# At a step's boundary the waiting probabilities are split ahead of Q's last evacuation; sums of the ffn weights, loads of x and splits of the first tiles are moved

## The chip, the cores and the metric

One core of a Trainium2 chip runs the whole program. The time is the device time of one execution in microseconds; lower is better. The number to predict is the median over runs of the changed kernel, timed on the same chip as the kernel before. Engines are called PE (matmuls), PEld (its weight loads), ACT, DVE, POOL and SP (SP only issues transfers and waits).

## What is computed

The reference, cut to what matters (B = 8 batches of S = 512 rows, D = 1024, 16 heads of 64):

```python
q, k, v = proj(x, Wq), proj(x, Wk), proj(x, Wv)      # float32, per head
q = q * minimum(cond_1, 4.0)
scores = einsum('bhqd,bhkd->bhqk', q, k) / 8.0
attn = softmax(where(causal, scores, finfo.min))
o = einsum('bhqk,bhkd->bhqd', attn, v)  # then heads side by side
y = einsum('bsd,ed->bse', o, Wo)
scale_x = maximum(max(abs(y), axis=-1), 1e-5) / 127
q_x = clip(round(y / scale_x), -128, 127) * scale_x
alpha = maximum(mean(abs(weight)), 1e-5)
q_w = clip(round(weight / alpha), -1, 1) * alpha
return x + einsum('bsi,oi->bso', q_x, q_w) + bias
```

## The kernel before

All float32 matrices are split in two parts ("high" is the value rounded by ACT to the multiplier's format, "low" is what is left, written by DVE or POOL), and each product is made of three matmul passes. So every operand costs a high operation on ACT and a low one on DVE or POOL before PE may use it. The order of the instructions on each engine is written out by hand; engines meet in semaphores, each engine takes its own instructions strictly in order, and SP issues every transfer but one in the order in which it is written.

**Stage V** (to 333 us) computes V for all rows. Pairs of row tiles n = 0 and 1 are done plainly; n = 2 to 15 are done in seven products each (A11, S4, A12, S2, S1, S3, A22, in this order on PE, 12 matmuls each, function `v_product`). PSUM bank `bank_z` is used by A12, then S1, then A22: S1 waits until DVE has added A12's result (`v_sum(n, 0)`), A22 waits for ACT's copy of S1's (`v_copy(.., V_TMP_R)`). S3 waits for the copy `V_TMP_U`. Beside the products of pair n, ACT and DVE split the seven operands of pair n + 1 (`xv_split`: B11, B22, B21, T2, T1, T3, T4), and DVE's `v_sum(n, 0)` stands behind its low parts of B11 and B22. Results go to HBM by `store_v`; the high part `v_high(n, q)` waits until the store that last used its slot has landed.

In the same stage the ffn weight is made ternary. SP loads its eight slices (`load_wf`, 512 KB each, two buffers): slices 0 and 1 at the end of pair 2, slices 2 and 3, 4 and 5, 6 and 7 at the end of pairs 3, 4 and 5, each time behind the pair's last `store_v`. ACT sums their absolute values (`wf_abs`, two at the end of each of the pairs 3 to 6); PE adds over the partitions (`wf_add_partitions`, line 942, in pair 7 behind A11); DVE forms alpha (`wf_scale`) and then rounds one slice a pair in three operations (`wf_ternary`, parts 0 to 2), which are spread over the pair's DVE work. At the end of pair 15, ACT also splits Wq's and Wk's first group and the eight slices of the first x tile (`x_high(act, 0, k)`).

**Stage A** (333 to 1600 us) has 32 steps, 4 groups of 4 heads by 8 batches, and a closing one. A step's PE program (`pe_step`) projects K and Q for the step `now` (`J(gi, k)`, four groups K0, Q0, K1, Q1 of 8 slices, lines 174) and between them does scores `S(u)`, transposes `T(u)` and products with V `PV(h)` of 16 units u = (head, row tile), some of the step `old`, the later ones of `now`. A unit goes: S(u) on PE, mask and row minimum on DVE (`M`, line 254), exponential on ACT (`E`, line 261), reciprocal on DVE (`I`), normalising on POOL (line 273), T(u) on PE, then the transposed probabilities are split, high on ACT (`H`, line 297) and low on DVE (`L`, line 304). T(u) waits for L(u - 2), since there are two PSUM banks.

The **boundary** of a step: PE ends a step with S(5), T(2), J(3, 7) and starts the next with S(6), T(3), J(0, 0..1), S(7), T(4), J(0, 2..3), S(8), T(5). J(3, 7) completes Q1; at the head of the next step ACT copies it out in two halves with the scale (`evac_hi(act, o, 3)`, line 204), DVE writes its low parts (`evac_lo(dve, o, 3)`, line 219) and the next scale (`batch_scale`), and behind these stand H(2) and L(2). S(8) is the first unit of the second head pair: it waits for these evacuations and for `k_sw`, the copy of K1 with the halves swapped, which SP makes by two transfers (`swap_k(.., 1)`, lines 229 and 230). SP issues them at the head of its step, behind `store_o(.., 1)` of the step that ended, which waits for the last addition of the output, OA(3) on DVE. The x slices of the next step are split at the end of a step: ACT 0 to 5 in three pairs (4 and 5 as the step's last work), DVE 0, 2, 4, POOL 1, 3, 5 behind units 2, 3 and 4; slices 6 and 7 follow inside the next step. `load_x` is issued behind `swap_k(.., 1)` of each step; in the very first step, which has no `old`, it is the first thing SP issues, ahead of the swap of K0 (`swap_k(.., 0)`) for which S(0) waits.

**Stage F** (from about 1600 us) multiplies with Wo, quantises, transposes and multiplies with the ternary weight, 32 row tiles. The first two tiles' splits (`o_high`, `o_low_part`), Wo's slices (`wo_high`, `wo_low`) and part of their products (`YY(k)`, `Y`) lie inside the last steps of stage A.

## Time and profile before

| | |
|---|---|
| median of 3 runs | 2084.48 us (2084.17 to 2085.92) |
| the profiled execution's own time | 2085.09 us |
| its span in the profile | 2083.3 us, mean granted clock of PE 0.994 of full speed |
| PE busy | 1991.5 us (96%) |
| DVE, ACT, POOL busy | 1416.1, 1114.4, 888.4 us |
| idle time of PE in stage A at T(4), behind DVE's L(2) | about 1.26 to 1.74 us in most steps |
| time from one boundary to the next | 38.4 to 38.7 us in most steps |

Busy times say which engine is near its limit over the whole; what a change of order can bring is read from PE's idle time and from what ended it, and at each place from the time at which the next thing in the chain becomes ready. In the rows, an instruction's line gives its start and length in us, its engine and line, what it writes and reads, and in brackets how long the engine had been idle before it and who ended that. `x12` are twelve instructions merged into one row.

### The profile page before, as it was taken

The page shows a single profiled execution, that of the slowest core. Times are in us where ns is not written, and L with a number is a line of the kernel's source. Part 1 is how long each engine was busy: PE and PEld are TensorE (multiplying, and loading weights), DVE is VectorE, ACT ScalarE, POOL GpSimd, SP SyncE. Part 2 cuts the span into 40 slices and gives each one's busy share as a digit, 9 for nine tenths or more (in the row PEclk, how much of TensorE's full clock was granted, in tenths as well). Part 3 has the DMA queues.
Part 4 walks back from the last instruction along what each step waited for, and adds up shares of the span by engine and source line. Part 5 has one row for each costly group of instructions (what it writes and reads, how often), then busy time and mean ns, then how long its engine had stood idle before and what let it go on. Part 6 is the DMA issues. An engine that isn't in the chain of part 4 may idle for free.

```text
span 2083.3 us, 34749 instructions
## 1 busy us (share of the span) xinstructions
PE 1991.5 (96%) x10074; PEld 1617.8 (78%) x10074; DVE 1416.1 (68%) x3277; ACT 1114.4 (53%) x2497; POOL 888.4 (43%) x816
## 2 busy tenths in 40 slices
PE   8999998999999999999999999999997999999998
PEld 6877886788788788787788787787886777777775
DVE  6667774777778777778777778777777554545454
ACT  4554444777767677768777778777775000000000
POOL 0343332544444444444444445444444544444442
PEclk9999999999999999999999999999999999999999
DMA  6666555333453443453433443433443423232322
GB/s 206 222 220 210 200 176 181 122 125 101 146 156 102 135 128 101 144 159 102 147 116 106 151 151 103 151 110 111 146 147 96 146 91 121 91 121 91 121 91 81
DMA packets 200981, 282.43 MB, mean 136 GB/s; under 512 B 11216, under 2 KB 146384, under 8 KB 199760
## 3 DMA queue, kind: packets, MB, share of 16 engines
q1 hardware_dynamic: 200384, 281.07, 42.8%
q8 instruction: 34, 0.56, 0.1%
q10 hardware_dynamic: 528, 0.52, 0.1%
q14 instruction: 35, 0.29, 0.0%
HBM read 178.79 MB, written 69.21 MB: 119 GB/s over the span
## 4 chain that ended last, share of the span: by engine, by line
PE 72%; DVE 10%; issue 6%; ACT 6%; DMA 3%; POOL 1%; DVEq 0%; SPq 0%; ACTq 0%; POOLq 0%
PE proj_ps L174 24%; PE proj_ps L509 8%; PE s_ps L509 8%; PE o_ps L317 6%; PE o_ps L580 5%; PE t_ps L870 5%; PE t_ps L283 5%; PE o_ps L870 3%; PE s_ps L243 2%; PE s_ps L242 2%; DVE q_st L219 2%; ACT parts L359 2%; DVE prob L254 2%; DVE parts L365 1%; ACT prob L261 1%
## 5 line engine op out<-in xcount | busy, mean ns | idle before, releaser
L174 PE MATMUL proj_ps<-parts 128*128 128x512 f32 x3072 | 840.9, 408 | 0.0
L273 POOL TENSOR_TENSOR prob<-prob,row_inv 128x128 f32<-128x128 f32 (+3 forms) x512 | 387.6, 757 | 696.2 <-DVE row_inv L267 691.2
L174 PEld LDWEIGHTS proj_ps<-parts 128*128 128x128 f32 x3072 | 540.6, 190 | 95.8
L261 ACT ACTIVATE prob<-prob,row_min 128x128 f32<-128x128 f32 (+3 forms) x512 | 287.7, 562 | 176.7 <-DVE row_min L254 171.4
L254 DVE CUSTOM_DVE_ANT_0 prob<-s_ps,mask 128x128 f32<-128x128 f32 (+3 forms) x512 | 248.2, 485 | 58.5 <-PE s_ps L243 25.2
L283 PE MATMUL t_ps<-ident,prob 128*128 128x128 f32 x1280 | 228.2, 277 | 53.1 <-DVE pt_lo L304 50.8
L297 ACT ACTIVATE pt_hi<-t_ps 128x128 fp32r<-128x128 f32 (+3 forms) x512 | 220.1, 430 | 107.6 <-PE t_ps L283 104.5
L565 ACT ACTIVATE yt_q<-t_ps 128x1024 bf16<-128x1024 bf16 x32 | 32.7, 1023 | 427.1 <-PE t_ps L558 427.1
L304 DVE TENSOR_TENSOR pt_lo<-t_ps,pt_hi 128x128 fp32r<-128x128 f32 (+3 forms) x512 | 249.1, 487 | 17.7 <-ACT pt_hi L297 12.1
L283 PEld LDWEIGHTS t_ps<-ident,prob 128*128 128x128 f32 x1280 | 152.4, 141 | 77.8 <-DVE pt_lo L304 44.5
L365 POOL TENSOR_TENSOR parts<-x_raw,parts 128x512 fp32r<-128x512 f32 x128 | 192.3, 1503 | 17.7 <-ACT parts L359 17.7
L509 PE MATMUL proj_ps<-parts,o_parts 128*128 128x512 f32 x768 | 188.5, 400 | 4.2 <-POOL o_parts L487 4.2
L509 PE MATMUL s_ps<-parts,o_parts 128*128 128x512 f32 x768 | 185.6, 397 | 0.0
L509 PEld LDWEIGHTS proj_ps<-parts,o_parts 128*128 128x128 f32 x768 | 143.9, 190 | 35.1 <-POOL o_parts L487 4.4
L242 PE MATMUL s_ps<-k_sw,q_st 128*128 128x128 f32 (+3 forms) x512 | 160.3, 313 | 7.5 <-issue 5.0
L509 PEld LDWEIGHTS s_ps<-parts,o_parts 128*128 128x128 f32 x768 | 143.3, 189 | 30.6
L243 PE MATMUL s_ps<-k_st,q_st 128*128 128x128 f32 (+3 forms) x512 | 166.0, 324 | 0.0
L317 PE MATMUL o_ps<-pt_lo,v_st 128*128 128x512 f32 (+3 forms) x512 | 161.2, 326 | 2.7 <-DVE pt_lo L304 2.7
L267 DVE RECIPROCAL row_inv<-row_sum 128x1 f32<-128x1 f32 x512 | 82.6, 161 | 115.5 <-ACT prob L261 112.1
L334 DVE TENSOR_TENSOR o_sum<-o_ps,o_low 64x512 f32<-64x512 f32 x128 | 87.4, 683 | 89.0 <-ACT o_low L326 88.8
L359 ACT ACTIVATE parts<-x_raw 128x512 fp32r<-128x512 f32 x256 | 146.0, 618 | 3.1 <-DMA x_raw<-xT 2.2
L317 PE MATMUL o_ps<-pt_hi,v_st 128*128 128x512 f32 (+3 forms) x512 | 147.0, 324 | 0.0
(118 smaller groups left out, 2891.3 us busy)
## 6 DMA issues: line engine op xcount, KB each, us to landing
x_raw<-xT SPq DMA_DIRECT2D x128, 512.0 KB, 5.5
v_scratch<-v_out SPq DMA_DIRECT2D x64, 512.0 KB, 3.3
k_sw<-k_st SPq DMA_DIRECT2D x128, 256.0 KB, 3.7
v_st<-v_scratch SPq DMA_DIRECT2D x128, 256.0 KB, 2.7
oT_scratch<-o_sum SPq DMA_DIRECT2D x64, 256.0 KB, 2.1
x_raw<-oT_scratch SPq DMA_DIRECT2D x32, 512.0 KB, 4.7
x_tile<-x SPq DMA_DIRECT2D x32, 512.0 KB, 5.3
out<-res SPq DMA_DIRECT2D x32, 512.0 KB, 3.2
```

The lines of the kernel that those rows point to most:

```text
L174: mm = pe.matmul(out, l, r, start=(k == 0 and i == 0), stop=(k == KT - 1 and i == 2))
L242: pe.matmul(s_ps[u % 2][:, 0:w], q, k_sw[:, h, 0:w], start=True, stop=False)
L243: pe.matmul(s_ps[u % 2][:, 0:w], q, k_st[:, h, 0:w], start=False, stop=True).then_inc(s_done, 1)
L254: dve.tensor_tensor_reduce(prob[:, u % 4, 0:w], s_ps[u % 2][:, 0:w], mask[:, S - w:S], 1.0, -MASKED, ALU.add, ALU.min, row_min[:, u % 4:u ...
L261: act.activation(prob[:, u % 4, 0:w], prob[:, u % 4, 0:w], ACT.Exp, bias=row_min[:, u % 4:u % 4 + 1], scale=-1.0, accum_out=row_sum[:, u % ...
L273: pool.tensor_tensor(prob[:, u % 4, 0:w], prob[:, u % 4, 0:w], row_inv[:, u % 4:u % 4 + 1].broadcast_to([P, w]), ALU.mult).then_inc(norm_d ...
L283: mm = pe.transpose(t_ps[u % 2][:, kb * P:(kb + 1) * P], prob[:, u % 4, kb * P:(kb + 1) * P], ident[:, :])
L297: act.activation(pt_view(pt_hi[h % 2], qt), t_ps[u % 2][:, 0:(qt + 1) * P] .rearrange("p (k q) -> p k q", q=P), ACT.Copy).then_inc(pt_hi_d ...
L304: dve.tensor_tensor(pt_view(pt_lo[h % 2], qt), t_ps[u % 2][:, 0:(qt + 1) * P] .rearrange("p (k q) -> p k q", q=P), pt_view(pt_hi[h % 2], q ...
L317: mm = pe.matmul(o_ps[h % 2][:, q0:S], v, part[h % 2][:, kb, q0:S], start=(kb == 0 and part is pt_lo), stop=(kb == QT - 1 and part is pt_hi))
L365: eng.tensor_tensor(x_lo[:, k, :], x_raw[:, k, :], x_hi[:, k, :].bitcast(F32), ALU.subtract).then_inc(x_lo_done[k % 2], 1)
L509: mm = pe.matmul(y_ps[p][half][:, :], a[p][:, o], b[k][:, w], start=(k == 0 and i == 0), stop=(k == KT - 1 and i == 2))
```

## The change

In stage V: the sums of absolute values of the ffn weights are taken from the end of pairs 3 to 6 into them (the even slice behind the high part of B11, the odd one behind that of T3); PE's sum over the partitions stands behind A12 of pair 7 and not behind A11; DVE's scale and rounding parts stand later within a pair, part 0 behind T2, part 1 behind T3, part 2 behind T4. In pair 15 ACT splits x slices 0 to 3 at the old place and 4 to 7 behind the copy `V_TMP_R`.

At the boundary: ACT does H(2), and DVE L(2), ahead of Q1's evacuation. The x slices 4 and 5, split at the end of a step before, are split at the head of the next (ACT and DVE; POOL's slice 5 ahead of its first unit). In the first step the load of the next x is issued behind the swap of K0 and the first two loads of V. In the last steps the first two tiles of the output are split one step earlier, without the wait for the projections' end.

The diff:

```diff
--- before.py
+++ after.py
@@ -474,7 +474,6 @@
             if due(count := (t - p) * 8 + 16):
                 eng.wait_ge(o_in[p], count)
             if isinstance(t, int) and t < 2:
-                eng.wait_ge(x_free, STEPS * KT)
                 eng.activation(o_hi[p], o_raw[p], ACT.Copy).then_inc(o_hi_done, 1)
             else:
                 if due(count := 2 * t - 2):
@@ -932,6 +931,8 @@
             sp.dma_start(wf_tmp[n % 2], wf[:, n % KT, :]).then_inc(wf_in[n % 2], 16)
 
         def wf_abs(act, k):
+            if not 0 <= k < KT:
+                return
             act.wait_ge(wf_in[k % 2], (k // 2 + 1) * 16)
             act.activation(wf_tmp[k % 2], wf_tmp[k % 2], ACT.Abs, accum_out=wf_sums[:, k:k + 1])\
                .then_inc(wf_abs_done, 1)
@@ -1017,10 +1018,10 @@
             v_plain(pe)
             for n in range(PLAIN, PAIRS):
                 v_product(pe, n, A11)
+                v_product(pe, n, S4)
+                v_product(pe, n, A12)
                 if n == WF_FROM:
                     wf_add_partitions(pe)
-                v_product(pe, n, S4)
-                v_product(pe, n, A12)
                 v_product(pe, n, S2)
                 v_product(pe, n, S1)
                 v_product(pe, n, S3)
@@ -1062,6 +1063,7 @@
             for n in range(PLAIN, PAIRS):
                 v_copy(act, n, V_TMP_A)
                 xv_split(act, n + 1, B11, False)
+                wf_abs(act, 2 * (n - WF_ABS_FROM))
                 if n == PAIRS - 1:
                     for gi in range(4):
                         split_w_qk(act, -1, 0, gi, False)
@@ -1070,20 +1072,21 @@
                 v_high(act, n, 0)
                 v_copy(act, n, V_TMP_U)
                 if n == PAIRS - 1:
-                    for k in range(KT):
+                    for k in range(4):
                         x_high(act, 0, k)
                 xv_split(act, n + 1, T2, False)
                 v_copy(act, n, V_TMP_R)
+                if n == PAIRS - 1:
+                    for k in range(4, KT):
+                        x_high(act, 0, k)
                 xv_split(act, n + 1, T1, False)
                 xv_split(act, n + 1, T3, False)
+                wf_abs(act, 2 * (n - WF_ABS_FROM) + 1)
                 v_high(act, n, 1)
                 v_high(act, n, 2)
                 v_copy(act, n, V_TMP_P)
                 xv_split(act, n + 1, T4, False)
                 v_high(act, n, 3)
-                if WF_ABS_FROM <= n < WF_ABS_FROM + KT // 2:
-                    for k in range(2):
-                        wf_abs(act, 2 * (n - WF_ABS_FROM) + k)
 
         def v_dve(dve):
             for i, (k0, k1) in enumerate(V_PIECES):
@@ -1120,9 +1123,6 @@
             for n in range(PLAIN, PAIRS):
                 xv_split(dve, n + 1, B11, True)
                 xv_split(dve, n + 1, B22, True)
-                if n == WF_FROM:
-                    wf_scale(dve)
-                wf_ternary(dve, n - WF_FROM, 0)
                 if n == PAIRS - 1:
                     batch_scale(dve, 0, 0)
                     split_w_qk(dve, -1, 0, 0, True)
@@ -1130,18 +1130,20 @@
                 v_sum(dve, n, 0)
                 xv_split(dve, n + 1, B21, True)
                 v_low(dve, n, 0)
-                wf_ternary(dve, n - WF_FROM, 1)
                 xv_split(dve, n + 1, T2, True)
+                if n == WF_FROM:
+                    wf_scale(dve)
+                wf_ternary(dve, n - WF_FROM, 0)
                 if n == PAIRS - 1:
                     split_w_qk(dve, -1, 0, 2, True)
                     split_w_qk(dve, -1, 0, 3, True)
                     x_low(dve, 0, 0)
                     x_low(dve, 0, 2)
                 xv_split(dve, n + 1, T1, True)
-                wf_ternary(dve, n - WF_FROM, 2)
                 v_sum(dve, n, 1)
                 v_sum(dve, n, 2)
                 xv_split(dve, n + 1, T3, True)
+                wf_ternary(dve, n - WF_FROM, 1)
                 if n == PAIRS - 1:
                     x_low(dve, 0, 4)
                     x_low(dve, 0, 6)
@@ -1149,6 +1151,7 @@
                 v_low(dve, n, 2)
                 v_sum(dve, n, 3)
                 xv_split(dve, n + 1, T4, True)
+                wf_ternary(dve, n - WF_FROM, 2)
                 v_low(dve, n, 3)
 
         def v_pool(pool):
@@ -1319,12 +1322,13 @@
                 if ending:
                     wo_high(act, k)
 
+            H(2)
             if old:
                 evac_hi(act, o, 3)
-            if ending:
-                o_high(act, 0, 0)
-            H(2)
             WO(2)
+            if now and old:
+                x_high(act, n, 4)
+                x_high(act, n, 5)
             E(5)
             if now and old:
                 x_high(act, n, 6)
@@ -1347,8 +1351,6 @@
             WO(6)
             H(7)
             E(10)
-            if ending:
-                o_high(act, 1, 1)
             H(8)
             E(11)
             WO(7)
@@ -1374,6 +1376,7 @@
             E(2)
             X(0, 1)
             if last and now:
+                o_high(act, 0, 0)
                 wo_high(act, 0)
             W(2)
             H(0)
@@ -1384,7 +1387,8 @@
             H(1)
             E(4)
             OL(3)
-            X(4, 5)
+            if last and now:
+                o_high(act, 1, 1)
 
         def dve_step(dve, old, now, nxt, qk_for=None, late_for=None, last=False):
             o, n, x = old and old[0], now and now[0], nxt and nxt[0]
@@ -1429,14 +1433,15 @@
                 if ending:
                     wo_low(dve, k)
 
+            L(2)
             if old:
                 evac_lo(dve, o, 3)
                 if now:
                     batch_scale(dve, n, now[2])
-            L(2)
             I(5)
             M(6)
             if now and old:
+                x_low(dve, n, 4)
                 x_low(dve, n, 6)
             WO(2)
             L(3)
@@ -1509,33 +1514,34 @@
             I(4)
             OA(3)
             M(5)
-            X(4)
 
         def pool_step(pool, old, now, nxt, qk_for=None, late_for=None, last=False):
             o, n, x = old and old[0], now and now[0], nxt and nxt[0]
             ending = last and not now
-            if ending:
-                o_low_part(pool, 0, 0)
+            if now and old:
+                x_low(pool, n, 5)
             for u in range(5, UNITS):
                 if old:
                     normalise(pool, o, u)
                 if u == 5 and now and old:
                     x_low(pool, n, 7)
-                if u == 10 and ending:
-                    o_low_part(pool, 1, 1)
             if ending:
                 split_o(pool, 2, 0)
             if now:
                 for u in range(5):
                     normalise(pool, n, u)
-                    if nxt and 2 <= u:
+                    if nxt and 2 <= u < 4:
                         x_low(pool, x, 2 * u - 3)
+                    if last and u == 3:
+                        o_low_part(pool, 0, 0)
+                if last:
+                    o_low_part(pool, 1, 1)
 
         def sp_step(sp, old, now, nxt, qk_for=None, late_for=None, last=False):
             ending = last and not now
             if old:
                 swap_k(sp, old[0], 1)
-            if nxt:
+            if nxt and old:
                 load_x(sp, *nxt)
             if qk_for is not None:
                 load_w(sp, qk_for)
@@ -1567,6 +1573,7 @@
                     sp.wait_ge(slot, PAIRS * 2 * 16)
                 load_v(sp, *now, 0)
                 load_v(sp, *now, 1)
+                load_x(sp, *nxt)
             if now:
                 load_v(sp, *now, 2)
             if now:
```

## Rows read from the trace of the kernel before

**Rows 1.** Waits of PE: who waited for whom, us in total, times, longest; two stretches.

```profile
PE t_ps L283 <- DVE pt_lo L304: 44.2, 31, 2.6
...
PE o_ps L870 <- ACT v_tmp L881: 1.5, 2, 0.9
```

**Rows 2.** Timeline of one boundary, all engines: start, length, engine, line.

```profile
909.36 0.94 PE L174 MATMUL proj_ps<-parts 128*128 128x512 f32 x3
...
911.03 1.39 ACT L204 ACTIVATE q_st<-proj_ps,q_scale 64x512 fp32r<-64x512 f32 x2
...
913.50 0.56 DVE L304 TENSOR_TENSOR pt_lo<-t_ps,pt_hi 128x384 fp32r<-128x384 f32 x1
...
914.20 0.30 PE L283 MATMUL t_ps<-ident,prob 128*128 128x128 f32 x1 [1.26 <-DVE pt_lo L304]
...
915.29 0.68 DVE L304 TENSOR_TENSOR pt_lo<-t_ps,pt_hi 128x512 fp32r<-128x512 f32 x1
...
916.11 0.41 PE L283 MATMUL t_ps<-ident,prob 128*128 128x128 f32 x2
```

**Rows 3.** The same boundary: the swap's second transfer and S(8); landing of all such.

```profile
911.87 0.59 SPq L230 DMA_DIRECT2D k_sw<-k_st  x1
...
915.62 0.19 PEld L242 LDWEIGHTS s_ps<-k_sw,q_st 128*128 128x128 f32 x1 [0.15 <-DMA k_sw<-k_st]
...
DMA to landing us min/median/max: 3.7/3.7/13.2
```

**Rows 4.** Timeline of another boundary: low parts of x on POOL and DVE.

```profile
716.44 1.30 POOL L365 TENSOR_TENSOR parts<-x_raw,parts 128x512 fp32r<-128x512 f32 x1
...
716.47 1.82 DVE L365 TENSOR_TENSOR parts<-x_raw,parts 128x512 fp32r<-128x512 f32 x1
```

**Rows 5.** Timeline of stage V: loads of the ffn weight, their landing, ACT, DVE, PE.

```profile
80.55 1.12 SPq L932 DMA_DIRECT2D x_raw<-wf  x2
...
101.19 1.32 SPq L932 DMA_DIRECT2D x_raw<-wf  x2
...
158.38 1.30 SPq L932 DMA_DIRECT2D x_raw<-wf  x2
...
DMA to landing us min/median/max: 4.6/5.8/6.3
...
79.67 1.41 ACT L788 ACTIVATE xv<-xv_raw 128x512 fp32r<-128x512 f32 x2
...
99.96 1.04 ACT L936 ACTIVATE x_raw<-x_raw 128x1024 f32<-128x1024 f32 x1
...
83.16 0.69 DVE L899 TENSOR_TENSOR v_tmp<-t_ps,v_tmp 128x512 f32<-128x512 f32 x1 [0.23 <-PE t_ps L870]
...
85.68 2.88 PE L870 MATMUL t_ps<-wv_last,xv 128*128 128x512 f32 x12
88.40 2.88 PE L870 MATMUL o_ps<-wv_last,xv 128*128 128x512 f32 x12
...
159.37 0.39 PE L942 MATMUL s_ps<-wf_sums,ones 128*128 128x8 f32 x2 [3.43 <-ACT x_raw L936]
```

**Rows 6.** Timeline of stage V's end and the first step; the first swap's landing.

```profile
325.66 2.38 ACT L359 ACTIVATE parts<-x_raw 128x512 fp32r<-128x512 f32 x4 [0.80 <-DMA x_raw<-xT]
...
328.67 4.48 PE L870 MATMUL t_ps<-wv_last,xv 128*128 128x512 f32 x12 [2.84 <-ACT v_tmp L881]
...
352.97 0.45 PE L242 MATMUL s_ps<-k_sw,q_st 128*128 128x128 f32 x1 [4.85 <-issue]
...
DMA to landing us min/median/max: 9.1/9.1/9.1
```

**Rows 7.** PE in two stretches: its busy time (matmuls), granted clock, DMA share, GB/s.

```profile
329.00:331.00 2.00, 2.00 (x6) 0.50 0.00 0
...
161.00:165.00 4.00, 4.00 (x20) 1.00 0.99 292
```

**Rows 8.** Timeline of the closing step: PE's wait for the first output tile.

```profile
1574.30 2.93 PE L509 MATMUL proj_ps<-parts,o_parts 128*128 128x512 f32 x6 [4.21 <-POOL o_parts L487]
```

## The prediction

> **What bounds the kernel now.** I read the page first: PE is busy 96% of the span, so only its 90 us of idle time and its slow stretches can be won, and only what makes PE wait can lose. So the waits of PE come next, then, at each place that the change touches, the timeline of all engines. In stage A nearly every wait of PE is one at T(4) for DVE's L(2): between 410 and 1560 us 31 of them, 44.2 us together [rows 1]. In stage V there are two waits for ACT's copy of A11's result (1.5 us) [rows 1] and one of 3.43 us for the sums of absolute values [rows 5]; at its end one of 2.84 us before A22 and one of 4.85 us before S(0) [rows 6]; in the closing step one of 4.21 us for the first tile's low part [rows 8].
>
> **The boundary of a step, 31 times.** L(2) stands behind both halves of Q1's evacuation: ACT starts that at 911.03, DVE's L(2) starts at 913.50, T(4) at 914.20 after 1.26 us of idle time [rows 2]. After the change H(2) and L(2) need only T(2) and M(5), both there by 911.0, so L(2) ends at about 911.5 and T(4) no longer waits. That gives 1.26 us at this place, and some 40 us if nothing else were late. But something is. S(8) needs `k_sw`. Its second transfer is issued at 911.87 and lands 3.7 us later, at 915.57; PE's weight load for S(8) starts at 915.62 and had been idle 0.15 us for just this [rows 3]. SP issues the transfer behind `store_o`, which waits for OA(3); nothing ahead of OA(3) on ACT or DVE is changed. I looked at all boundaries: in 23 of 31 S(8) starts within 0.3 us of the landing. So the stall only moves from T(4) to S(8), and the most that the swap of L(2) can give is what lies between landing and S(8) in the other boundaries (2.0 us in one, 0.7 in three, under 0.3 in the rest but the first).
>
> T(5) needs L(3), which ended at 915.97; T(5) started at 916.11 [rows 2]. Is L(3) later now? J(3, 7) ends at 909.36 + 0.94 = 910.30 [rows 2]. ACT does H(2) until then, Q1's high part to 911.74, slices 4 and 5 (1.04) to 912.8, E(5) with its read of the sum (0.6) to 913.4; before, E(5) ended at the same time, since the slices only stood elsewhere. DVE reaches I(5) at 913.3 and waits 0.1 for it, does M(6) to 914.0, then two low parts, slices 4 and 6, where one was. A low part of x on DVE and one on POOL do not run together: the DVE operation at 716.47 takes 1.82 us, and it ends 0.55 us after POOL's of 716.44 has ended [rows 4]; alone a DVE operation of this size takes 0.69 [rows 5]. POOL's slice 5 runs from 912.9 to 914.2 (1.3), its normalising of unit 5 (0.6) comes between the two of DVE. So slice 4 ends at 914.8, slice 6 at 915.8 and L(3) at 916.4 instead of 915.97. T(5) is late by 0.45 us at this boundary. At the others the same working gives 0 to 0.3, as S(8) or the evacuation was later there: 26 boundaries together +5.0 us, the other four together -2.9. Sum **+2.1 us**; bounds: no loss from the two low parts -3, half a microsecond at each of 30 boundaries less the same 3 us +12. I take +2.1, since the row of the boundary itself gives it.
>
> The Trainium skill (SBUF — State Buffer, SBUF: two separate sides) says that this port pair is an exclusive lock held for the whole instruction, so the loser blocks. The rows agree. It says nothing on who gets it next; if DVE's second operation always went ahead of POOL's, L(3) would be 0.6 us earlier than I say and the boundary would cost nothing, which is the lower bound above.
>
> **Sums of the ffn weights, stage V.** Removed: PE's 3.43 us before line 942 (with the restart of the stream 3.9 us from the end of A11 to S4), and the two waits for the copy (with the products around them 2.1 us), both because ACT had two sums of 1.04 + 0.19 us each at a pair's end ahead of `v_copy`. So -6.0 us.
>
> Added: the even sum now stands on ACT between the high parts of B11 and B22 of the next pair, and it waits for its slice in ACT's own queue. What is queued behind it: B22's and B21's high parts, `v_high(n, 0)`, `v_copy(U)`; who waits for those: DVE's B22 low, behind it in order `v_sum(n, 0)`, and for this PE's S1. In pair 3 ACT has B11's part done at about 80.2 (79.67 is B11 and B22 together) [rows 5]. Slice 0 is issued at 80.55 and the fastest landing of such a load is 4.6 us [rows 5], so it is there at 85.13. From there: sum 1.23, B22 high 0.6, B22 low 0.7, `v_sum` 0.69: 88.4. S1 starts at 85.68 now and products follow each other in 2.72 us [rows 5]. PE stalls **2.8 us**.
>
> Pairs 4, 5 and 6 have the same pattern, since slices 2, 4 and 6 are issued only behind the last `store_v` of the pair before. That issue came at 101.19 where pair 4 began at 93.84 (85.68 + 3 x 2.72), 7.35 us in, and at 158.38 where pair 7 began at 159.37 - 3.43 - 2.88 = 153.06, 5.3 us in [rows 5]. The landing takes 4.6 to 6.3, median 5.8 [rows 5]; the work from landing to `v_sum` takes 3.25; S1 is wanted 4 x 2.72 = 10.88 us in. Stall: at least 5.3 + 4.6 + 3.25 - 10.9 = 2.3, at most 7.35 + 6.3 + 3.25 - 10.9 = 6.0; I take 3.4 (issue at 5.7, as ACT no longer does two sums ahead of the next copy, landing 5.4). Together 2.8 + 3 x 3.4 = **13.0 us**, bounds 9.7 and 20.8. The odd sums stand behind T3 and find their slice landed: nothing, but for half a microsecond on `store_v`, which is in the 5.7.
>
> These stalls have a second price. After the idle 2.84 us before A22 the granted clock is 0.50, that is 1.2 GHz, and A22 takes 4.48 us where the others take 2.72 [rows 6, 7]; of seven idle times of 2.6 to 4.9 us of PE inside the program six were followed by such a stretch, each costing some 1.7 us, and one was not: after 3.43 us the clock stayed at 1.00 [rows 5, 7]. For four stalls I take three slow stretches, 5.2 us; bounds 0 and 7. The later places of scale and rounding on DVE cost nothing: behind T2 and T3 DVE waits for ACT anyway (over 1 us a pair), and S1 and S4 have 2 us and more of cover. Stage V: -6.0 + 13.0 + 5.2 = **+12.2 us**, bounds +4 and +22.
>
> **The end of stage V and the first step.** A22 waits for the copy R because ACT does x slices 4 to 7 first, which arrive until 326.9 [rows 6]. After: slices 0 to 3 end at 324.9, the copy at 325.5, A22 starts at 325.8. Back come 2.84 and the slow clock's 1.76: -4.6. S(0) waits 4.85 us for `k_sw` [rows 6], whose transfer needs 9.1 us behind 2 MB of x where 3.7 is the usual time [rows 3, 6]. After, the swap goes first: K0's low part at about 338.1, landing 342.5, S(0) wanted at 343.5. -4.85. The load of x then lands from 346 to 353, ACT wants it from 349 on: covered. From S(0) to T(5) of the next step the kernel before needs 18.57 us at a slow clock. At full clock ACT and DVE bound it (V(2), E, M, the split slices in order): 17.2 by the same durations. -1.35. Sum **-10.8 us**, bounds -5.5 (the swap late by 3, the rest not gained) and -13.
>
> **The end of stage A.** YY(0) waited 4.21 us for POOL's low part [rows 8]. Early splitting makes it ready, then PE waits for Q1's evacuation until 1572.2: 2.1 us won. But T(5) then waits for H(3), which stands on ACT behind a slice of Wo that lands at 1576.2 as before; 0.9 are left, and the chain of Wo's loads (load, high, low, next load) keeps 0.7 of it. **-0.7**, bounds -3 (the slow stretch goes too) and +2 (a new one comes).
>
> **Sum.** 12.2 - 10.8 + 2.1 - 0.7 = +2.8 us. Against the profiled execution (2085.1, a span of 2083.3 and 1.8 around it) 2087.9; it lay 0.6 above the median, so on the median of 2084.5: **2087.3 us**.
>
> **Rivals.** (1) The moved stall pays: if `k_sw` landed earlier once PE is earlier, each boundary gives up to its 1.3 us, 31 x 1.3 = 40 us: 2084.5 - 40 + 12 - 11 - 1 = about 2045. For it only the 1.26 us of idle time; against it rows 3. Chance 0.07. (2) The sums find their slices: the store's landing and the issue come earlier than I think, and stalls are a third. Then stage V is -6 + 4 = -2 and the whole 2084.5 - 2 - 10.8 + 1.4 = 2073. The loads' fixed place behind `store_v` speaks against it. 0.14. (3) Slower: DVE and POOL queue for their port with three low parts in the first 4 us of each step, so that L(3) is late by 0.9 us and not by 0.2; it decides from the point at which L(3) ends 0.35 us behind the landing, which it does at most boundaries already. 30 x 0.6 more: 2087.3 + 18 = 2105. 0.13. (4) The order is as I say and sizes hold: 0.66, own range 2080 to 2096.
>
> **Chances and range.** About 0.2% (4.2 us) is what a measurement can tell from no change. Of case 4, 0.29 lies above 2088.7, 0.33 within and 0.04 below 2080.3. With the rivals: faster 0.04 + 0.07 + 0.13 = 0.24, same 0.34, slower 0.29 + 0.13 = 0.42. The range from 2074 to 2099 leaves out rival 1, most of 3 and a part of 2, and takes in stage V's bounds but for the last few microseconds.
>
> **What the profile after would show.** Right: no idle time at T(4), 1.2 to 1.5 us at S(8) released by the swap or at T(5) by L(3); four waits at S1 of pairs 3 to 6 of 2.5 to 4 us for `v_sum`, granted clock 0.50 behind most; no waits at line 942, A22, S(0). Wrong: boundaries less than 38.4 us apart (rival 1), or over 39 us (rival 3); S1 without waits (rival 2).

## The result, and the profile after

The kernel after takes **2134.15 us** (median of 4 runs, 2131.74 to 2138.23), the kernel before in the same comparison 2085.2; the ratio is 1.0235, with an interval from 1.0216 to 1.0254. The forecast was 2087.3 with a range from 2074 to 2099: the change costs 49 us where +2.8 was forecast, and the time lies far outside the range. The profiled execution has a span of 2136.4 us. It is the slowest of the four (2138.23), 53 us above the profiled execution of the kernel before (2085.09); the shares that are read from it below are shares of these 53.

Its first lines, from the page: PE is busy 38 us longer than in the kernel before (1991.5 us), with the same number of matmuls.

```profile
span 2136.4 us, 34723 instructions
## 1 busy us (share of the span) xinstructions
PE 2029.9 (95%) x10074; PEld 1649.6 (77%) x10074; DVE 1411.3 (66%) x3277; ACT 1112.6 (52%) x2497; POOL 883.8 (41%) x816
```

The waits of PE over the whole program (who waited for whom; us in total, times, longest) answer [rows 1]:

```profile
PE s_ps L242 <- DMA k_sw<-k_st: 46.4, 30, 2.1
PE t_ps L283 <- DVE pt_lo L304: 22.8, 36, 2.1
PE t_ps L869 <- DVE v_tmp L898: 12.2, 4, 3.4
```

The stall of T(4) has gone and stands at S(8), released by the swap, 30 times; the second line is now mostly T(5), and the third the four waits of S1 in stage V that the prediction asked for. The same boundary as in [rows 2, 3], here of another step (start, length; the idle time before it and its releaser in brackets), first PE:

```profile
1095.19 1.64 PE L174 MATMUL proj_ps<-parts 128*128 128x512 f32 x6
...
1097.13 0.27 PE L283 MATMUL t_ps<-ident,prob 128*128 128x128 f32 x1
...
1100.44 0.32 PE L242 MATMUL s_ps<-k_sw,q_st 128*128 128x128 f32 x1 [1.64 <-DMA k_sw<-k_st]
...
1101.17 0.41 PE L283 MATMUL t_ps<-ident,prob 128*128 128x128 f32 x2 [0.30 <-DVE pt_lo L304]
```

and what DVE, POOL and SP did:

```profile
1095.26 0.55 DVE L304 TENSOR_TENSOR pt_lo<-t_ps,pt_hi 128x384 fp32r<-128x384 f32 x1
...
1097.96 0.16 DVE L267 RECIPROCAL row_inv<-row_sum 128x1 f32<-128x1 f32 x1 [0.29 <-ACT prob L261]
...
1098.72 1.70 DVE L365 TENSOR_TENSOR parts<-x_raw,parts 128x512 fp32r<-128x512 f32 x2
1100.35 0.68 DVE L304 TENSOR_TENSOR pt_lo<-t_ps,pt_hi 128x512 fp32r<-128x512 f32 x1
...
1098.77 1.10 POOL L273 TENSOR_TENSOR prob<-prob,row_inv 128x256 f32<-128x256 f32 x1
...
1096.52 0.59 SPq L230 DMA_DIRECT2D k_sw<-k_st  x1
```

T(4) starts at 1097.13, in the stream of products, as L(2) was done at 1095.81. So PE reaches S(8) earlier, but the swap is issued where it was and S(8) waits 1.64 us. PE then has 0.43 us of work and waits another 0.30 for L(3). And now the view that the prediction did not ask for at this place, PE's granted clock around it (us, PE busy, PEclk, DMA share, GB/s):

```profile
1090.00:1098.00 8.00, 8.00 (x47) 1.00 0.32 90
1098.00:1102.00 4.00, 2.06 (x11) 1.00 0.29 82
1102.00:1106.00 4.00, 4.00 (x15) 0.57 0.70 220
1106.00:1130.00 24.00, 24.00 (x132) 1.00 0.36 116
```

Behind the pair of waits the granted clock is 0.57 on the mean of four us: part of them ran at 1.2 GHz. In the record of the granted clock such a slow stretch is 3.41 us long here. I counted the boundaries with one within 8 us of T(4), the first of the 31 boundaries left out: 1 of 30 before, **23 of 30** after. From T(5) to the next T(5) it is 39.0 us where no slow stretch lies between them and 40.57 where one does; before it was 38.56. (Every eighth step is longer in both kernels, 40.7 us before.)

That gives two terms. From T(5) of the first of 31 boundaries to T(5) of the last (stage A, for short) the kernel took 1165.3 us and takes 1212.7, 47.4 more. Idle time of PE in it was 50.1 us and is 63.5: +13.3, or 30 x (39.0 - 38.56). The other 34 are the clock. Of the 23 boundaries one has its stretch behind the last T(5), outside stage A, and one has a stretch of double length (6.83 us), so stage A holds 23 slow lengths where it held one: 22 x (40.57 - 39.0) = 34.5. The stretch behind the last boundary adds 1.6 more; the rest of the 53 us lies ahead of stage A (2.4) and behind it.

Stage V, where [rows 5] stood:

```profile
88.64 4.58 PE L869 MATMUL t_ps<-wv_last,xv 128*128 128x512 f32 x12 [3.23 <-DVE v_tmp L898]
...
112.94 1.62 PE L869 MATMUL t_ps<-wv_last,xv 128*128 128x512 f32 x3 [3.39 <-DVE v_tmp L898]
...
137.00 2.47 PE L869 MATMUL t_ps<-wv_last,xv 128*128 128x512 f32 x5 [3.28 <-DVE v_tmp L898]
...
159.94 2.49 PE L869 MATMUL t_ps<-wv_last,xv 128*128 128x512 f32 x6 [2.25 <-DVE v_tmp L898]
```

Four stalls of S1, 12.15 us together; the first has its cause in ACT's queue (the even sum waits for its slice, and B22's high part stands behind it):

```profile
85.50 1.06 ACT L937 ACTIVATE x_raw<-x_raw 128x1024 f32<-128x1024 f32 x1 [5.64 <-DMA x_raw<-wf]
86.46 0.19 ACT L937 ACTIVATION_READ_ACCUMULATOR x_raw<-x_raw 128x1 f32 x1
86.55 1.13 ACT L787 ACTIVATE xv<-xv_raw 128x512 fp32r<-128x512 f32 x2
```

At the end of stage V ([rows 6]) the wait before S(0) is gone, and that before A22 is 0.61 us where it was 2.84. The closing step ([rows 8]) keeps 2.61 of its 4.21 us:

```profile
1624.47 2.67 PE L508 MATMUL proj_ps<-parts,o_parts 128*128 128x512 f32 x6 [2.61 <-issue]
```

### The profile page after: what moved, and what is told of

It is laid out like the page before. It is cut to its first block, busy times and chain, and to the rows that moved or that the text cites. A ratio compares the mean times of both kernels' runs of the same rounds, so it can differ in the third digit from the quotient of the medians.

```text
span 2136.4 us, 34723 instructions
## 1 busy us (share of the span) xinstructions
PE 2029.9 (95%) x10074; PEld 1649.6 (77%) x10074; DVE 1411.3 (66%) x3277; ACT 1112.6 (52%) x2497; POOL 883.8 (41%) x816
## 4 chain that ended last, share of the span: by engine, by line
PE 70%; DVE 10%; issue 8%; ACT 8%; DMA 3%; ACTq 1%; DVEq 0%; SPq 0%; POOL 0%; POOLq 0%
PE proj_ps L174 23%; PE proj_ps L508 8%; PE s_ps L508 8%; PE o_ps L317 6%; PE t_ps L869 5%; PE o_ps L579 5%; PE t_ps L283 5%; PE o_ps L869 4%; ACT parts L359 3%; DVE parts L365 2%; PE s_ps L243 2%; PE s_ps L242 2%; DVE prob L254 2%; ACT prob L261 2%; DVE pt_lo L304 1%
## 5 line engine op out<-in xcount | busy, mean ns | idle before, releaser
L174 PE MATMUL proj_ps<-parts 128*128 128x512 f32 x3072 | 858.4, 414 | 0.0
L273 POOL TENSOR_TENSOR prob<-prob,row_inv 128x128 f32<-128x128 f32 (+3 forms) x512 | 397.0, 776 | 688.2 <-DVE row_inv L267 683.2
L174 PEld LDWEIGHTS proj_ps<-parts 128*128 128x128 f32 x3072 | 549.7, 193 | 101.7
L365 POOL TENSOR_TENSOR parts<-x_raw,parts 128x512 fp32r<-128x512 f32 x128 | 182.7, 1428 | 70.7 <-ACT parts L359 70.7
L242 PE MATMUL s_ps<-k_sw,q_st 128*128 128x128 f32 (+3 forms) x512 | 160.6, 314 | 46.6 <-DMA k_sw<-k_st 46.4
L283 PEld LDWEIGHTS t_ps<-ident,prob 128*128 128x128 f32 x1280 | 152.4, 141 | 41.5 <-issue 28.3
L317 PE MATMUL o_ps<-pt_lo,v_st 128*128 128x512 f32 (+3 forms) x512 | 172.1, 346 | 2.7 <-DVE pt_lo L304 2.7
L242 PEld LDWEIGHTS s_ps<-k_sw,q_st 128*128 128x128 f32 x512 | 96.5, 188 | 79.9 <-issue 47.0
L317 PE MATMUL o_ps<-pt_hi,v_st 128*128 128x512 f32 (+3 forms) x512 | 157.2, 343 | 0.0
```

The lines of the kernel that those rows point to most:

```text
L174: mm = pe.matmul(out, l, r, start=(k == 0 and i == 0), stop=(k == KT - 1 and i == 2))
L242: pe.matmul(s_ps[u % 2][:, 0:w], q, k_sw[:, h, 0:w], start=True, stop=False)
L273: pool.tensor_tensor(prob[:, u % 4, 0:w], prob[:, u % 4, 0:w], row_inv[:, u % 4:u % 4 + 1].broadcast_to([P, w]), ALU.mult).then_inc(norm_d ...
L283: mm = pe.transpose(t_ps[u % 2][:, kb * P:(kb + 1) * P], prob[:, u % 4, kb * P:(kb + 1) * P], ident[:, :])
L317: mm = pe.matmul(o_ps[h % 2][:, q0:S], v, part[h % 2][:, kb, q0:S], start=(kb == 0 and part is pt_lo), stop=(kb == QT - 1 and part is pt_hi))
L365: eng.tensor_tensor(x_lo[:, k, :], x_raw[:, k, :], x_hi[:, k, :].bitcast(F32), ALU.subtract).then_inc(x_lo_done[k % 2], 1)
```

## The experiments

**Which part costs.** Five kernels each hold one part of the change, or all but one. The first has only the two edits at the boundary:

```diff
+            H(2)                         # ACT; DVE the same with L(2)
             if old:
                 evac_hi(act, o, 3)
...
-            H(2)
             WO(2)
+            if now and old:              # slices 4 and 5 here, not at the
+                x_high(act, n, 4)        # end of the step before; DVE and
+                x_high(act, n, 5)        # POOL with them
...
-            X(4, 5)
```

> The kernel before with the change at the boundary alone (H(2) and L(2) first, x slices 4 and 5 at the head of the next step); stage V, the first step's load and the closing steps stay. Theory, the clock: PE's idle time moves from T(4) to S(8) and grows by the wait at T(5), to 1.9 us within about 2.5 us, and the granted clock is 0.50 behind most boundaries (24 of 31 in the changed kernel, each 3.4 us long, so 1.7 us lost each, 41 us) plus 0.2 us of waits at each: 2085 + 41 + 6 = about 2132 us. Rival, the port: only the waits count, 31 x 0.5 = 15 us, 2100 us, and the rest of the 49 us is elsewhere.

Measured: 2137.3, ratio 1.0236 [1.0219, 1.0253]. The whole loss is here, with slow stretches behind 22 of 30 boundaries. Its profiled execution (2136.64) splits the loss in the same way: stage A takes 1211.8 us, 46.5 more than before, of which 13.3 are idle time (63.4 us) and 33 the clock. The counterpart has everything but these edits:

> The changed kernel with the boundary of the steps as before. Theory, the clock at the boundary: 2085 + 49 - 47 = 2087 us, within 3; the four waits at S1 stay (12.2 us together, each followed by a clock of 0.50). Rival, the loss is in stage V and its clock: 2115 or more.

Measured: 2087.7 against 2087.67, ratio 1.0001 [0.9991, 1.001]. Stage A takes 1165.4 us, as before. So all else in the change cancels out, within 2 us. Its terms, one at a time; first only the sums of stage V (the even sum behind B11, the odd one behind T3, scale and rounding later):

> The kernel before with the ffn weight's part of the change alone: sums of absolute values within pairs 3 to 6, PE's sum over partitions behind A12, scale and rounding later. Theory (the sum of the prediction): -6.0 for the waits removed, +12.2 for four waits at S1 as in the changed kernel (3.2, 3.4, 3.3, 2.3 us), and +6.8 for four slow stretches: +13 us, 2098 us. Rival, the sums cost nothing net: 2085 us, and the first step gives nothing either.

Measured: 2099.42, +11.6 us, ratio 1.0051 [1.0034, 1.0068]. Then only the end of stage V and the first step:

> The kernel before with x slices 4 to 7 of the first tile split behind the copy R, and the load of the second x tile behind the first swap. Theory: A22 and S(0) no longer wait and the clock stays up: -10.8 us, 2074 us. Rival, the gain is taken back in the first step, where DVE and the arrival of x come next: -5 us or less.

Measured: 2074.6, -13.2 us, ratio 0.9934 [0.9918, 0.9951]. And only the end of stage A:

> Only the end of stage A changed (first two output tiles split early). The prediction said -0.7 us, so 2086.9 to 2087. The comparison of the kernels with all but the boundary, the sums alone and the start alone leaves +2 us for it: 2089.

Measured: 2087.78 against 2087.53, ratio 1.0 [0.999, 1.0009]: nothing that can be told from none.

**Which of the two edits.** Only H(2) and L(2) first:

> The kernel before with H(2) and L(2) ahead of Q1's evacuation and nothing else; slices 4 and 5 stay at the end of a step. Theory: PE's idle time moves from T(4) to S(8), which waits for the swap's landing as before; L(3) ends when it did, so T(5) has no wait of its own. Idle time per boundary stays 1.3 to 1.5 us, the clock stays at 1.00, and the time is 2085 us, within 3. Rival, the swap of the two alone does the harm (a wait at S(8) costs the clock, one at T(4) doesn't): 2085 + 40 = 2125 us.

Measured: 2092.78, ratio 1.0025 [1.0013, 1.0037]. The stall has moved (waits of PE between 400 and 1560 us):

```profile
PE s_ps L242 <- DMA k_sw<-k_st: 43.2, 29, 2.1
```

and slow stretches stand behind three of 30 boundaries, all among the first five, where S(8) waits 1.75 to 2.07 us; later it waits 0.8 to 1.7 and there is none. So the expectation of no cost missed by 5 us, in the direction of the clock. A boundary of it, beside the one of the change above: the same wait at S(8), none at T(5), and no slow stretch behind it.

```profile
1117.16 0.32 PE L242 MATMUL s_ps<-k_sw,q_st 128*128 128x128 f32 x1 [1.64 <-DMA k_sw<-k_st]
...
1117.43 0.41 PE L283 MATMUL t_ps<-ident,prob 128*128 128x128 f32 x2
```

Only the slices 4 and 5 moved:

> The kernel before with x slices 4 and 5 split at the head of the next step and nothing else; L(2) stays behind the evacuation. Theory: L(2) comes 0.6 us earlier, since ACT starts the evacuation 0.7 us earlier; PE idles 0.6 us at T(4), 0.6 at S(8) and 0.3 to 0.5 at T(5), since L(3) stands behind one more low part and POOL's operations: 0.3 us more per boundary, 8 us, 2093 us, and more by 1.7 us for each boundary at which this idle time brings the clock down, up to 2130. Rival, the slices are harmless: 2085 us.

Measured: 2110.54, ratio 1.011 [1.0093, 1.0127]. This one is the most telling. PE idles *more* than in the full change, 68.6 us in stage A (18.5 more than before, where the expectation had 8), but at each boundary in three pieces:

```profile
1083.38 0.33 PE L283 MATMUL t_ps<-ident,prob 128*128 128x128 f32 x1 [0.76 <-DVE pt_lo L304]
1083.47 1.66 PE L174 MATMUL proj_ps<-parts 128*128 128x512 f32 x6
1085.78 0.33 PE L242 MATMUL s_ps<-k_sw,q_st 128*128 128x128 f32 x1 [0.65 <-DMA k_sw<-k_st]
...
1087.03 0.41 PE L283 MATMUL t_ps<-ident,prob 128*128 128x128 f32 x2 [0.81 <-DVE pt_lo L304]
```

and no boundary of the 30 is followed by a slow stretch. Between the first piece and the second stand 1.7 us of products, between the second and the third only S(8) with 0.4 us. So of the 2.2 us of a boundary 1.46 stand close together, about as much as the single wait of the kernel before, and the clock stays; 1.94 us so placed, as in the change, lose it. The sum of idle time over a boundary does not decide. Alone the two edits cost 5 and 23 us, together 50, though the idle time of stage A grows less with both (13.3) than with the slices alone (18.5): the many slow stretches come only with both.

**Is it the swap?** The full change with the second swap (`swap_k(.., 1)`) issued a good part of a step earlier, so that `k_sw` has long landed:

```diff
-            if old:
-                swap_k(sp, old[0], 1)
...
             if now:
                 load_v(sp, *now, 2)
+                swap_k(sp, now[0], 1)
```

> The changed kernel with SP's swap of K1 issued behind the third load of V of its own step, so that it lands well before S(8). Theory: the wait at S(8) goes (46 us), but T(5) still waits for L(3), which hangs on the evacuation and the two low parts; PE's idle time of 1.9 us stands in one piece at T(5), the clock still falls behind most boundaries, and the time stays at 2130 to 2137. Rival, the swap is what holds the boundary back: T(4) and S(8) are both free and the time falls to about 2134 - 46 - 35 = 2053 us, as my rival 1 had it.

Measured: 2134.24, ratio 1.022 [1.0203, 1.0237]; the same time as the change itself. S(8) no longer waits, T(5) takes all of it over:

```profile
1098.02 0.33 PE L242 MATMUL s_ps<-k_sw,q_st 128*128 128x128 f32 x1
...
1100.34 0.41 PE L283 MATMUL t_ps<-ident,prob 128*128 128x128 f32 x2 [1.88 <-DVE pt_lo L304]
```

Slow stretches stand behind 22 boundaries. So in the change L(3), behind Q1's evacuation and the two low parts, is what sets the boundary, and the swap only landed just ahead of it. What the early swap would bring without the slices at the boundary was not run alone.

**Is it the length of the wait, or its new place?** In the runs so far waits of 1.9 us stood at S(8) and T(5), the waits of 1.4 us of the kernel before at T(4). To hold the place and change the length, tiny DVE operations (128x1, into a tile that nothing reads) go ahead of L(2) in the kernel before:

```diff
                     batch_scale(dve, n, now[2])
+                    for i in range(12):   # 3, 6, 12 or 20
+                        dve.tensor_scalar(unused[:, i:i + 1], cond_bc[:, 0:1], 4.0, 1.0, ALU.min, ALU.mult)
             L(2)
```

> The same with three operations: the wait at T(4) about 1.7 us, +10 us of idle time in all. Where the new place is what matters: 2098. Where the length is: the waits of 1.75 us in the kernel with only L(2) first were followed by a low stretch in three of five cases, those of 1.65 and less in none of 24, so between 0 and 15 low stretches, 2098 to 2122; I expect some five, 2105.

> The kernel before with six tiny DVE operations (128x1, some 0.11 us each in a row) between Q1's evacuation and L(2), so that the wait at T(4) grows from about 1.4 to about 2.05 us at each of 30 boundaries, in the place where the kernel before has it. Idle time alone: 30 x 0.66 = +20 us. Theory (the clock falls where PE idles about 1.9 us or more in one stretch, wherever it stands): low stretches behind 15 or more of the 30 boundaries, 1.6 us each, so +44 to +68 us, 2132 to 2156. Rival (only the new place of the waits, at S(8) and T(5), makes the clock fall): a handful of low stretches as before, 2108.

Measured: 2092.18, ratio 1.0026 [1.0017, 1.0036], and 2096.85, ratio 1.0045 [1.0028, 1.0061]. The doses came out smaller than meant: 12 such operations take 0.81 us (below), not 1.3, so most waits were 1.53 and 1.72 us, and both times fell under what was expected. Slow stretches behind 2 and 1 of 30. Place and length are not told apart by that, so larger doses followed:

> The kernel before with twelve tiny DVE operations ahead of L(2). Six made the wait at T(4) 1.72 us (0.055 each), so twelve make it about 2.05. Idle time alone: 30 x 0.66 = +20 us, some of it taken back as S(8) waits less: 2105. If the length of one wait decides, as the waits of 1.88 to 1.93 us in the changed kernel suggest, the clock falls behind 15 or more boundaries, each 1.6 us: 2129 to 2153. If the place decides, 2105 and up to five low stretches.

> The same with twenty operations: a wait of about 2.5 us at T(4), idle time alone 30 x 1.1 = +33 us: 2118. By length: low stretches behind most boundaries, 2118 + 20 to 30 x 1.6 = 2150 to 2166. By place: 2118.

Measured: **2136.57**, ratio 1.0235 [1.0213, 1.0257], and 2157.43, ratio 1.0332 [1.0315, 1.0349]. With twelve operations the kernel before is as slow as the kernel after. One boundary of it, PE and DVE, and the clock:

```profile
1098.53 0.33 PE L284 MATMUL t_ps<-ident,prob 128*128 128x128 f32 x1 [2.10 <-DVE pt_lo L305]
...
1097.09 0.81 DVE L1438 TENSOR_SCALAR unused<-cond_bc 128x1 f32<-128x1 f32 x12
...
1097.00:1099.00 2.00, 0.47 (x3) 1.00 0.64 174
1099.00:1102.40 3.40, 3.40 (x14) 0.62 0.06 11
```

The step from six operations to twelve adds 9.7 us of idle time in stage A (59.2 to 69.0) and 40 us of time. What came in between is in the table; the waits are those of most boundaries, in us, the last column the boundaries of 30 that a slow stretch follows.

| kernel | T(4) | S(8) | T(5) | idle, stage A | time | slow |
|---|---|---|---|---|---|---|
| before | 1.4 | 0 to 0.15 | 0 to 0.1 | 50.1 | 2085.2 | 1 of 30 |
| + 3 operations | 1.53 | 0 | 0.05 | 53.5 | 2092.18 | 2 |
| + 6 | 1.72 | 0 | 0.09 | 59.2 | 2096.85 | 1 |
| + 12 | 2.10 | 0 | 0 | 69.0 | 2136.57 | 23 |
| + 20 | 2.60 | 0 | 0 | 83.6 | 2157.43 | 28 |
| L(2) first | 0 | 1.2 to 1.8 | 0 | 52.8 | 2092.78 | 3 |
| slices 4, 5 moved | 0.75 | 0.6 | 0.85 | 68.6 | 2110.54 | 0 |
| after | 0 | 1.6 | 0.3 | 63.5 | 2134.15 | 23 |
| after, swap early | 0 | 0.05 | 1.88 | 64.9 | 2134.24 | 22 |

The table gives the usual wait, and the rare stretches stand behind waits that are longer than usual. In the kernel before the one stands behind 2.64 us; with three operations both stand behind 1.89 us; with six the one stands behind the wait of 1.88 shown here, and none behind the 26 waits of about 1.71:

```profile
686.11 0.33 PE L284 MATMUL t_ps<-ident,prob 128*128 128x128 f32 x1 [1.88 <-DVE pt_lo L305]
```

A longer wait does not always bring one either: three of 2.07 to 2.08 us (six operations) and three of 2.44 (twelve) had none.

So the place is not needed, at T(4) the clock falls as well, and the rival is out. Idle time that stands close together is what the slow stretches follow, and about 0.4 us more of it per boundary turned a rare stretch into the rule.

**A boundary that works.** If L(3) is what comes last, the low parts of x must leave the first microseconds of the step. The next kernels put slices behind H(3) and L(3), keep L(2) first and the swap early. For the boundary alone:

```diff
+            H(3)
+            if now and old:              # DVE: behind L(3) and M(7)
+                x_high(act, n, 4)
+                x_high(act, n, 5)
+            E(6)
             if now and old:
                 x_high(act, n, 6)
                 x_high(act, n, 7)
-            WO(3)
-            H(3)
-            E(6)
...
```

> The kernel before with L(2) first, the swap of K1 issued a fifth of a step earlier, and x slices 4 to 7 all split behind H(3) and L(3): the boundary of the best kernel so far, alone. That one ended 17 us under the kernel with only the start changed; if the boundary gives it, this ends at 2071 (2087.8 less 17). If half of those 17 us is the closing step's, it ends at 2079.

Measured: 2074.3, ratio 0.9935 [0.9918, 0.9952]; 12.8 us won, between the two expectations. With the start and the end of stage A of the change, and of its edits in stage V only the later place of PE's line 942:

> A version made from what the runs showed: H(2), L(2) first; all of x slices 4 to 7 behind H(3) and L(3) (POOL's behind units 5 and 6); swap of K1 early; the first step's and the closing steps' parts of the change; PE's sum over the partitions behind A12 with the sums of absolute values where they were. Theory: DVE's chain to L(3) is short by both low parts, L(3) ends at 4.1 us behind J(3, 7) and T(5) has at most 0.2 us of wait, so each boundary gives 1.3 us: 2085 - 30 x 1.3 - 10.8 - 3.9 - 0.7 = 2030 us. Rival, something else of the boundary comes next (norm of unit 5, slice 4 for J(0, 4)) and takes back over half: 2055 us.

Measured: 2057.65, ratio 0.9853 [0.9836, 0.9869]: the rival's 2055. A new wait takes up what was won, the first product of J waiting for slice 4's low part (waits of PE, 400 to 1500 us):

```profile
PE proj_ps L174 <- DVE parts L365: 23.6, 28, 0.9
```

So slices 4 and 5 go back to the end of the step before, and only 6 and 7 are late:

> The best kernel so far (2057.65) with x slices 4 and 5 split at the end of the step before, where the kernel before has them, and only 6 and 7 behind H(3) and L(3). In the best so far PE waits 0.85 us for slice 4's low part at 28 boundaries, 23.6 us together. If slices at the old place are ready, that goes: 2057.7 - 23.6 = 2034. If slice 6's low part on DVE makes the next wait (I(6) and M(7) stand behind it), half of it stays: 2046.

Measured: **2046.91**, ratio 0.9803 [0.9787, 0.982], 40 us under the kernel before and 87 under the change. Of the 40 some 13 are the start's, measured alone above. Half of the wait stayed, as the second expectation had it, now for M(6) at S(8). No boundary is followed by a slow stretch. The last try takes M(6), H(3) and L(3) ahead of Q1's evacuation:

> The best kernel so far (2046.9) with H(3) put ahead of Q1's evacuation on ACT, and M(6) and L(3) ahead of it on DVE. There PE waits 0.54 us at S(8) for M(6) and 0.25 us at T(5) for L(3) at some 28 boundaries, 22 us together. If both were only order: 2047 - 22 = 2025. Rival: E(5) and I(5) come later by as much, and PE waits at T(5) for POOL's normalised unit 5 in their place: half stays, 2036, or nothing is won.

Measured: 2095.61, ratio 1.0045 [1.0029, 1.0061]: 49 us worse than the one before it, where both expectations had a gain or none.

```profile
1066.38 0.32 PE L242 MATMUL s_ps<-k_sw,q_st 128*128 128x128 f32 x1 [0.62 <-DVE q_st L219]
...
1067.85 0.44 PE L283 MATMUL t_ps<-ident,prob 128*128 128x128 f32 x2 [1.03 <-POOL prob L273]
```

The wait for POOL is the rival's. The one for `q_st` is this edit's own: S(8) reads Q1, so Q1's evacuation is itself on PE's path once the swap is early. The two waits stand 0.4 us apart, and a slow stretch follows 13 of 30. Idle time in stage A grows by 25.6 us (28.3 to 53.9) and stage A by 46, so nearly half of this loss is again the clock, which neither expectation had.

## Why the prediction was wrong

**The failed step is the price of a boundary, and in it the clock.** The prediction found the order of events: no wait at T(4), the stall at S(8) for the swap, L(3) late for T(5) by the second low part. For stage V it counted the slow clock behind stalls, from [rows 6, 7]. For the boundaries, +2.1 us in its sum, it wrote only idle time, as if the granted clock stayed as it was so long as the idle time stayed nearly the same; the clock's term stood at nothing, without a reason. It had the rows to ask: its own count said that idle times of 2.6 us and more were mostly followed by a slow stretch, the waits of up to 1.74 us in the table above were not, and between these it had nothing. A bound from both sides would have put 0 to 30 x 1.7 = 51 us on the boundary, and the range would have held the time. The two edits together brought each boundary to 1.9 us in nearly one piece. Price: 33 to 34 us in stage A, and 1.6 behind it, some two thirds of the loss.

**The second error in the same step is the size of L(3)'s delay.** Forecast +0.45 us where it was worked out, and +2.1 us for all boundaries; measured 13.3. In the trace after, L(3) ends 6.37 us behind the end of J(3, 7) (1101.03 - 1094.66), forecast 6.1, before 5.67. ACT's evacuation, its slices and E(5) end 0.15 to 0.3 us later than worked out, M(6) on DVE 0.4; the two low parts, 1.70 us for both, took 0.1 less. The gain at T(4) was real, but it was spent in the same stretch; what is left is a loss of 0.44 us a boundary. The rival with late L(3) had this mechanism, at 0.6 us a boundary and 2105, with a chance of 0.13. Without the clock's fall the time would have been about 2085.2 + 13.3 = 2098.5, between case 4 and this rival and just inside the range.

The sentence on the exclusive port (the Trainium skill, SBUF — State Buffer, SBUF: two separate sides) is borne out so far as the rows go: POOL's normalising of a 128x256 tile, which overlaps DVE's low part, took 1.10 us here and 0.61 at the boundary of the kernel before. Of DVE's two low parts the first started ahead of POOL's normalising and took 0.69 us, the second

```profile
1099.32 1.10 DVE L365 TENSOR_TENSOR parts<-x_raw,parts 128x512 fp32r<-128x512 f32 x1
```

waited until POOL was done. So the engines took turns, the one that was already waiting going next; POOL's normalising came between DVE's two operations as the prediction had it, and the lower bound, for which DVE's second would have gone first, did not come about.

**The other terms held.** Sums of stage V: +12.2 forecast, +11.6 measured alone (interval 7 to 14); the stalls 13.0 forecast, 12.15 in the trace, the first of them 2.8 (2.7 by its own rows) against 3.23; and all four of them were followed by a slow stretch, not three, so that a little too much in one and too little in the other partly cancel. End of stage V and the first step: -10.8 forecast, -13.2 measured alone (interval -17 to -10). End of stage A: -0.7 forecast, 0.0 with an interval of some 2 us to either side. Together, without the boundary: +0.7 forecast, 0.0 measured, with 2 us to either side.

**Rival 1** (the moved stall pays, 2045) was rightly held unlikely as the code stood. But its reason was only half right: the prediction took the swap's landing for what bounds S(8) and, for this rival, looked no further. With the swap early nothing was won in the change, since L(3) took over the whole wait; in the kernel before, too, L(3) ended only 0.4 us behind the landing [rows 2, 3]. The kernel that took L(2), the swap and the slices out of the way won 12.8 us at the boundary alone.

## What to carry to other kernels

Where PE is nearly always busy, look up the granted clock behind each recurring wait, and give a change that lengthens or gathers such waits a term for it: 30 boundaries at 1.6 us are 48 us, as much as all waits at S(8) together (46.4). A moved stall is not a neutral one: ask what stands next to it, and lay new work of other engines where PE has products left, not into the microseconds in which it already waits. Before a wait is chased, list everything that ends within half a microsecond of its releaser: here the next of them took over what the removal of one had freed.

## What the runs showed of the hardware

- The granted clock fell behind waits far shorter than those of 2.6 to 4.9 us from which the prediction had it. Behind the 26 waits of 1.71 us at T(4) (six operations) it never fell, behind those of 2.10 us 23 times in 27, behind those of 2.60 us every time.
- Idle time in pieces counts less, if enough work stands between them: 2.2 us in three pieces, the first 1.7 us of products away from the others, none of 30.
- It is no clean function of the sum or of the longest piece. 0.62 and 1.03 us, with 0.4 us between, were followed by a slow stretch 13 times in 30, and single waits of 1.64 us at S(8) and of 1.71 us at T(4) never. Measured from the end of the products of J ahead of S(8) to the start of the next ones, the pause is about 2.1 us with only slices 4 and 5 moved (no stretch), 2.3 in the last try (13) and 2.5 in the change (23), which is in order; but the pause around T(4) with six operations is 2.26 us and had none. Why stays open.
- In the kernels with most stretches some boundaries with the same waits have none. With twelve operations the stretch starts 0.0, 0.5, 0.9 and 1.3 us behind T(4) at four boundaries in a row, the fifth has none, and the sixth begins again at 0.0: T(4) lies 40.5 us apart there, the starts of the stretches 40.96 (410.36, 451.31, 492.27, 533.23). With twenty operations, where T(4) lies 41.0 us apart, the starts are 40.96 apart too, and no boundary in such a row is left out. So the stretches keep a rhythm of their own against which the boundaries drift, and 23 of 30 is also a matter of where the boundaries fell.
- The Trainium skill (TensorE: Matmul & The Clock Gate, Part 1: The HAM clock gate) says that the gate's timing runs free and does not start anew with the kernel. The drift of the stretches agrees.
- A slow stretch cost 1.57 us of time in the change and with its swap early (40.57 against 39.0), 1.3 with twelve operations (40.5 against 39.2 from T(4) to T(4)).
- A DVE operation on 128x1 took 0.15 us alone, 12 in a row 0.81, 0.07 each.
- A low part of x (128x512) took DVE 0.69 us, and 1.10 where it waited for POOL; POOL's own took 1.30, and 1.72 behind DVE's.
